# A two-layer adaLN transformer on one core: modulation matrices and the identity are loaded first, later row blocks behind modulation products, and the first two LayerNorm chunks are transposed tile by tile

## What is computed

```python
mod = (_silu(L0_c) @ L0_wmod).reshape(L0_c.shape[0], 6, 1, -1)
sa, ca, ga, sb, cb, gb = (mod[:, 0], mod[:, 1], mod[:, 2], mod[:, 3], mod[:, 4], mod[:, 5])
...
h = _layernorm(x, axis=-1) * (1 + ca) + sa
x = x + ga * _L0_attn_ref(h, L0_attn_W_qkv, L0_attn_b_qkv, L0_attn_W_out, L0_attn_b_out)
h = _layernorm(x, axis=-1) * (1 + cb) + sb
x = x + gb * _L0_ffn_ref(h, L0_ffn_W1, L0_ffn_W2, L0_ffn_W3)
```

## Time and profile before

| | |
|---|---|
| median of 3 runs (lowest to highest) | 2014.23 us (2013.72 to 2018.39) |
| profiled execution, its time | 2016.38 us |
| its span, first to last instruction | 2014.6 us |
| TensorE busy (matmul) | 1929.0 us, 96% of the span |
| VectorE busy | 1089.8 us, 54% |
| ScalarE busy | 638.4 us, 32% |
| GpSimd busy | 542.2 us, 27% |
| mean granted TensorE clock | 0.987 |

### The profile page before, as it was taken

The page is one execution under the profiler, slowest core; times in us unless marked ns, Lnnn a source line. Parts: engine busy times, 40 slices in busy tenths (PEclk is TensorE's granted clock), DMA queues, the critical chain, the costliest instruction groups (busy, mean ns, idle before and its releaser), DMA issues. The chain is left out here.

```text
span 2014.6 us, 25805 instructions
## 1 busy us (share of the span) xinstructions
PE 1929.0 (96%) x10068; PEld 1389.3 (69%) x10068; DVE 1089.8 (54%) x1834; ACT 638.4 (32%) x1157; POOL 542.2 (27%) x521
## 2 busy tenths in 40 slices
PE   6999999999999998899999999999999889999998
PEld 4677545545555544688888888887886678888886
DVE  4456776676666748863434443445432774434334
ACT  3231355555555564431111211113321241121111
POOL 0122578788686468300000000002000510000000
PEclk9999999999999999999999999999999999999999
DMA  9644422322321203110000000002000011000002
GB/s 316 215 158 146 101 54 55 73 66 55 85 43 34 54 12 105 58 43 32 5 28 32 32 21 12 0 19 71 8 6 11 21 53 32 32 21 21 6 1 84
DMA packets 61722, 111.87 MB, mean 56 GB/s; under 512 B 6000, under 2 KB 21248, under 8 KB 61568
## 3 DMA queue, kind: packets, MB, share of 16 engines
q1 hardware_dynamic: 54144, 85.05, 14.5%
q0 software_dynamic: 7456, 25.18, 4.2%
HBM read 84.77 MB, written 25.44 MB: 55 GB/s over the span
## 5 line engine op out<-in xcount | busy, mean ns | idle before, releaser
L1218 DVE TENSOR_REDUCE part_max<-banks 128x1 f32<-128x512 f32 (+2 forms) x640 | 356.8, 612 | 152.4 <-PE banks L1190 94.1
L1718 ACT ACTIVATE probs<-banks 128x512 f32<-128x512 f32 (+3 forms) x640 | 310.9, 539 | 275.1 <-PE banks L1629 134.2
L1190 PE MATMUL banks<-kst,qst 96*128 96x512 f32 (+2 forms) x640 | 262.4, 419 | 12.7 <-DVE part_max L1218 9.5
L1629 PE MATMUL banks<-qst,kst 98*128 98x512 f32 (+2 forms) x640 | 252.0, 414 | 0.2 <-ACT probs L1718 0.2
L711 DVE TENSOR_TENSOR tokens_a<-banks,tokens_a 128x512 f32<-128x512 f32 x224 | 151.2, 687 | 70.0 <-PE banks L220 69.2
L738 DVE TENSOR_TENSOR tokens_b<-banks,tokens_b 128x512 f32<-128x512 f32 x64 | 44.2, 691 | 251.7 <-ACT tokens_b L653 251.6
L1586 POOL TENSOR_TENSOR early_weights<-probs 128x512 f32<-128x512 f32 (+2 forms) x152 | 160.4, 1084 | 66.5 <-ACT probs L1718 66.1
L218 PE MATMUL banks<-f_d_hi,f_hid_hi 128*128 128x512 f32 x432 | 170.1, 394 | 7.6 <-DVE tokens_a L711 5.2
L1586 POOL TENSOR_TENSOR pairs_own<-probs 128x512 f32<-128x512 f32 (+2 forms) x152 | 158.1, 1069 | 71.1 <-ACT probs L1718 70.9
L218 PE MATMUL banks<-h_hi,f_w_first 128*128 128x512 f32 x448 | 174.6, 390 | 0.0
L220 PE MATMUL banks<-h_hi,f_w_first 128*128 128x512 f32 x448 | 174.3, 389 | 0.0
(11 more groups left out here) (199 smaller groups left out, 3271.2 us busy)
## 6 DMA issues: line engine op xcount, KB each, us to landing
tokens_a<-in_L_wmod SPq DMA_DIRECT2D x12, 1024.0 KB, 7.3
qst<-q_hi SPq DMA_DIRECT2D x32, 256.0 KB, 5.9
kst<-k_hi SPq DMA_DIRECT2D x32, 256.0 KB, 8.0
x<-in_L_attn_x SPq DMA_DIRECT2D x4, 1024.0 KB, 13.0
q_hi<-qk_out_hi POOLq DMA_DIRECT2D x16, 256.0 KB, 3.0
q_lo<-qk_out_lo POOLq DMA_DIRECT2D x16, 256.0 KB, 3.2
k_hi<-qk_out_hi POOLq DMA_DIRECT2D x16, 256.0 KB, 4.1
k_lo<-qk_out_lo POOLq DMA_DIRECT2D x16, 256.0 KB, 4.2
```

Source lines behind the costliest of these rows:

```text
L1190: mm = nc.tensor.matmul(dst[:, 0:wide], qst[n % QS][0:BIASROW, h, P * t:P * t + P], kst[(NB * g + c) % KS][0:BIASROW, h, 0:wide], start=Tr ...
L1218: nc.vector.tensor_reduce(part_max[:, n % 2, ht, c:c + 1], max_bank(slot)[:, 0:wide], AX_X, ALU.max).then_inc(max_read, 1)
L1629: mm = nc.tensor.matmul(dst[:, c0:512], kst[ck % KS][0:BIASROW + 2, h, at:at + P], qst[n % QS][0:BIASROW + 2, h, c0:512], start=True, stop ...
L1718: nc.scalar.activation(probs[:, q % PS, h, c0:512], score_bank(sh)[:, c0:512], ACT.Exp, scale=SCALE).then_inc(exp_done, 1)
```

## The change

Six things are altered, all in the first stage.

1. SyncE's order: modulation matrix 0 comes first, then `picks`, matrix 1, the identity alone (64 KB), the first rows of x in two halves, the q weights. Matrix 2 (which waits for products(0)) comes before weights 1 and 2, and x block 1 after them. The rest of the constants follows. x blocks 2 and 3 stand behind `load_mod(6)` and `load_mod(8)`, so that they are issued only when products(4) and products(6) are done.
2. TensorE does products(0), products(1), sums(0), sums(1), where it did products, sums, products, sums. sums(1) has a bank of its own (5), and so does not wait for `mod_read`.
3. `first_tensor`: chunks 0 and 1 of block 0 are transposed tile by tile as z tiles become ready. Before, TensorE waited for all four tiles and for all constants.
4. VectorE copies only the identity ahead of the statistics (taken by halves); the four other copies of constants now stand between weights(1) and weights(2), behind a wait for the transfer of the constants.
5. ScalarE copies the modulation parts before `std_scalar(0)`, not after it.
6. TensorE waits for all constants (`const_ready`) only at item 6 of block 0.

```diff
+            def first_tensor(self, pe):
+                for t in range(TB):
+                    pe.wait_ge(self.z_ready, t + 1)
+                    for k in range(2):
+                        last = nc.tensor.transpose(self.turn_bank(k)[:, t * P:(t + 1) * P],
+                                                   self.z[:, 0, t, k * P:(k + 1) * P], ident[:])
+                        if t == TB - 1:
+                            last.then_inc(self.turned, 1)
...
-                load_x(0)
                 load_mod(0)
+                sp.dma_start(picks[:], a["const"][:, 8 * P:9 * P]).then_inc(picks_loaded, 16)
                 load_mod(1)
-                sp.dma_start(stage[:], a["const"][:, 0:6 * P]).then_inc(const_loaded, 16)
-                sp.dma_start(picks[:], a["const"][:, 8 * P:9 * P]).then_inc(picks_loaded, 16)
+                sp.dma_start(stage[:, 0:P], a["const"][:, 0:P]).then_inc(ident_loaded, 16)
+                for half in range(2):
+                    rows = slice(2 * half, 2 * half + 2)
+                    sp.dma_start(x0[:, rows, :], xt[:, rows, :]).then_inc(x_half_loaded[half], 16)
                 for k in range(KT):
                     sp.dma_start(w_raw[0][:, k, :], tile_rows(a["w_qkv"][0])[:, k, :]).then_inc(w_chunk_loaded[k], 16)
...
-                load_x(1)
+                load_mod(2)
                 sp.dma_start(w_raw[1], tile_rows(a["w_qkv"][1])).then_inc(w_loaded[1], 16)
                 sp.dma_start(w_raw[2], tile_rows(a["w_qkv"][2])).then_inc(w_loaded[2], 16)
-                load_x(2)
-                load_x(3)
-                for i in range(2, len(VECTORS)):
+                load_x(1)
+                sp.dma_start(stage[:, P:], a["const"][:, P:6 * P]).then_inc(const_loaded, 16)
+                for i in range(3, len(VECTORS)):
                     load_mod(i)
+                    if i in (6, 8):
+                        load_x(i // 2 - 1)
...
-                    else:
+                    elif i > 1:
                         pe.wait_ge(mod_read, i)
...
+                    if b == 0 and m == HALF:
+                        pe.wait_ge(const_ready, 1)
...
                 for i in range(2):
                     products(i)
+                for i in range(2):
                     sums(i)
-                pe.wait_ge(const_ready, 1)
-                norm.tensor(pe, 0)
+                pe.wait_ge(ident_ready, 1)
+                norm.first_tensor(pe)
+                norm.tensor(pe, 0, first=2)
...
-                norm.std_scalar(act, 0)
                 copy_parts(0)
                 copy_parts(1)
+                norm.std_scalar(act, 0)
...
-                dve.wait_ge(x_loaded[0], 16)
-                norm.stats_vector(dve, 0)
+                dve.wait_ge(ident_loaded, 16)
+                nc.vector.tensor_copy(ident[:], stage[:, 0:P]).then_inc(ident_ready, 1)
+                for half in range(2):
+                    dve.wait_ge(x_half_loaded[half], 16)
+                    norm.half_stats_vector(dve, 0, half)
+                norm.stats_vector(dve, 0, halves=())
                 norm.z_vector(dve, 0)
-                dve.wait_ge(const_loaded, 16)
-                nc.vector.tensor_copy(ident[:], stage[:, 0:P])
-                nc.vector.tensor_copy(ident16[:], stage[:, 0:P])
-                nc.vector.tensor_copy(hadamard[:], stage[:, P:2 * P])
-                nc.vector.tensor_copy(mask_keys[:], stage[:, 2 * P:4 * P])
-                nc.vector.tensor_copy(mask_queries[:], stage[:, 4 * P:6 * P]).then_inc(const_ready, 1)
                 take_sum(0)
                 take_sum(1)
                 weights(0)
                 norm.split_vector(dve, 0)
                 weights(1)
+                dve.wait_ge(const_loaded, 16)
+                nc.vector.tensor_copy(ident16[:], stage[:, 0:P])
+                nc.vector.tensor_copy(hadamard[:], stage[:, P:2 * P])
+                nc.vector.tensor_copy(mask_keys[:], stage[:, 2 * P:4 * P])
+                nc.vector.tensor_copy(mask_queries[:], stage[:, 4 * P:6 * P]).then_inc(const_ready, 1)
                 weights(2)
```

## The result

| | before | changed |
|---|---|---|
| median of 8 runs each | 2016.84 us | 2006.54 us |
| lowest to highest | 2011.71 to 2021.95 | 2000.49 to 2012.45 |
| ratio of the two, 95% interval | | 0.9943, 0.9921 to 0.9965 |
| profiled execution, its span | 2014.6 us | 1998.7 us |
| mean granted TensorE clock in it | 0.987 | 0.993 |

What follows compares the result with a forecast made beforehand. TensorE, busy 96% of the span, was taken as the bound, leaving 85.7 us idle plus lower-clock matmuls to win from. 9.6 us gained by item 2 less a 0.6 us wait gave 9.0, so 2005.2 us; 8-in-10 range 2003.0 to 2009.8.

Steps and rivals of the forecast that it cites:

- The bound and the order of loads: First loads: DMA engines full at 384 GB/s, so queue order sets landings, 2.7 us per 1 MB.
- The start: Start to item 0's first matmul: 20.7 us where it was 24.14, gain 3.4 us.
- VectorE therefore decides: Before item 0: VectorE's low parts of the q weights, ending at 20.0 us, set the first matmul at 20.7.
- Item 0 to item 2: Item 2 begins at 30.75 us instead of 40.39, gain 9.6: start 3.4, wait 4.2, clock 0.8 and 1.2.
- The clock's part: Products(2) and item 1 leave the lower clock level: 0.8 and 1.2 us of the 9.6.
- What is late next: At sums(3), TensorE waits 0.6 us for ScalarE's copy behind item 0's store, landing taken as 4.65 us; bounds 0 and 4.6.
- x behind the products at no cost: x blocks 2 and 3 travel while TensorE multiplies; cost between 0 and 2.0 us, taken as 0.
- The colder start: Rival, 0.14: less dense work before item 0 brings the lower clock, costing 2.0 and about 0.6 us; 2007.8 us.
- Stores that cost more than the change gives: Rival, 0.04: at 8.6 us landings, waits at first sums and items 4 and 6 lose 10.0 against 9.6; 2014.6 us.
- The rule I set aside: DMA queues take turns: a 256 KB store beside loads lands in 3.9 us, no wait, gain stays 9.6 us.
- The sum: Whole kernel: 9.6 - 0.6 = 9.0 us gained, lead kept to the end; 2005.2 us against the median 2014.23.

Runs made afterwards that it cites:

- e3: Changed kernel with x blocks 2 and 3 loaded at once behind the constants, ahead of matrix 3, not paced by products; 2014.53 us in one run.
- e4: Changed kernel with block 0's transposes as before, chunk by chunk after all four z tiles; 2008.36 us in one run.
- e5: Changed kernel with TensorE's order products(0), sums(0), products(1), sums(1) again, the bank of its own kept; 2006.75 us in one run.
- e1: Kernel before with one move: matrix 2 loaded ahead of x block 1 and weights 1 and 2; 2009.35 us in one run.
- e2: Changed kernel with the tail of the loads put back, matrix 2 behind x blocks 2 and 3, earlier start kept; 2016.72 us in one run.
- e6: Changed kernel with VectorE's copies of the constants and weights(2) moved behind item 0's output; 2000.47 us in one run.
- e9: Changed kernel with x blocks 2 and 3 issued behind matrices 8 and 9, not 6 and 8; 2007.85 us in one run.
- e7: From e6: matrix 4 issued only after item 1, constants behind it, VectorE's copies and weights(2) behind item 2's statistics hook; 2010.39 us in one run.
- e8: From e7: products(2) moved into item 0, behind its second chunk; ratio 0.9987 (0.9969 to 1.0006) to the kernel before, 12 runs.

## Why the prediction was right, and where it was not

**The bound and the order of loads: right.** Matrix 0 released TensorE at 6.97 us (predicted 7.2), the constants VectorE at 28.22 (28.2), matrix 3, issued at 18.7, landed 12.2 us later at 30.9 (30.9). Adding bytes at the measured 384 GB/s in queue order gave each within 0.3 us, though a first store, issued at 27.5, was on its way beside matrix 3. With four stores it failed: in e3 by some 4 us.

**The start: right in sum, half right in its cause.** Gain 3.4 predicted, 3.8 and 3.4 in the two pairs of traces. "VectorE therefore decides" fell: the low part began at 19.55, when ScalarE's high part (18.91 and 0.61) had just come, and e4 shows it waiting for ScalarE. Nor did I see that the start needed the table load hidden (e5).

**Item 0 to item 2: right.** Item 2 stood at 30.09 us (30.75 predicted), the gain there was 10.3 us, and 9.3 in the second pair of traces (9.6 predicted). e1 and e2 show the structure that the sum only assumed. By products(5) the start is worth nothing without the move, the move some 4 to 5 us without the start, and both together 8.7 to 9.9. The clock's part was sized from one trace; in the second trace of the kernel before the lower level was left sooner, and products(3) came 0.8 us earlier.

**What is late next: right place, wrong model, and the size by luck.** A wait at sums(3), released by ScalarE's copy, which waits for item 0's store: 0.6 us predicted, 0.52, 0.35 and 0 in three traces. But the terms were off and made up for each other. The store took 4.0, 4.1 and 3.5 us, not 4.65, which by my sum is a wait of about nothing; and TensorE wanted sums(3) at 37.0 us, 0.7 sooner than the 37.7 of the sum, which brought the wait back. Besides, I took the landing as a duration to be added to an issue time. e6 shows an issue 3.4 us earlier and the same landing.

**x behind the products at no cost: shown** by e9; that the pacing carries the whole gain (e3) was not in the prediction.

**The rivals.** The colder start did happen: item 0's first matmuls were 0.43 us apart in the changed kernel. It cost nothing: item 0 took 5.1 us (20.30 to 25.43) where it took 5.2, because it waits for its low parts in any case, and from the sixth matmul (22.55) on they had the length of the higher level. The Trainium skill ("TensorE: Matmul & The Clock Gate", the part on the clock gate) has the clock low unless activity keeps it up. The rows agree, here and behind each longer pause (e2: products of 1.93 us behind 8.59 us of idle time). Stores that cost more than the change gives did not come in the changed kernel, and came in e7 and e8.

**The rule I set aside.** The Trainium skill ("DMA: Bandwidth & Descriptors", queues, rings and completion order) has each DMA engine take turns between its queues. My estimate from it was that a 256 KB store beside loads lands in 3.9 us. For the store of the sum that came nearer than my 4.65 (4.0, 4.1 and 3.5 measured). But stores beside loads took up to 9.1 us here, and the same store took 7.6 in e6 and 8.7 in e8, so the fair share that I worked out is not what a store gets in general; why, no run here shows.

**The sum: right within the noise.** 9.0 us predicted, 2.0 of them from the clock; 8.0 measured at equal clock, 9.5 in the mean of all runs, 8.7 to 9.9 by products(5), 11.5 by the ratio of the first comparison. The 15.9 us between the first two spans are in part luck: the page's clock of 0.993 is the highest of all 27 runs of the changed kernel. What sets a run's clock in the stages that were not changed stays open.

## What to carry to other kernels

While the DMA engines are full, place loads by when each is first wanted, and take gains at the head of the program and in the order of loads as one: either alone can be worth nothing. Count stores into the same bandwidth, and don't treat a store's landing as a duration to add: issuing it earlier (e6) or moving a load out of its way (e7, e8) shifts the collision. Of the three attempts one gained nothing, and two reached products(5) 6.4 and 2.8 us later than the changed kernel. A long wait costs twice, once idle and once at the lower clock behind it (behind the 4.2 us of the earlier trace rows and the 2.49 of e8; behind the 0.94 of e1 the products ran at the higher level). When runs scatter by more than the effect, compare landmarks in traces, and set time against granted clock.

## What the runs showed that I had not expected

A 256 KB store took anything from 3.2 us (empty queue) to 9.1 us (e7, issued at 31.4 behind matrix 4 and the constants). ScalarE's table load of 1.28 us stood right ahead of the square root that needed it, and moved with the copy before it (12.49 us in the changed kernel, 13.94 in e5). And TensorE's granted clock, 0.984 to 0.993 as a mean over a run of the same program, goes with some 1.7 us of span for each 0.001.
